# Attention's projections, output product and running sum computed from split operands; the scores stay unsplit products in 32-row groups

## The chip, the cores and the metric

One core of a Trainium2 chip runs the whole program. The metric is the device time of one execution in microseconds (us), median of the runs. The core has five engines with queues of their own: TensorE (PE in the rows, its weight loads PEld), VectorE (DVE), ScalarE (ACT), GpSimd (POOL) and SyncE (SP), which here only issues DMAs. An engine takes its instructions strictly in the order in which they were written, and waits on semaphores where another engine or a DMA has to be done first.

## What is computed

```python
x = x + 0.5 * ffn(layernorm(x))        # x: (8, 1024, 512), fp32
x = x + attn(layernorm(x))
x = x + 0.5 * ffn(layernorm(x))

def attn(x):                            # 16 heads of 32
    q = exp(split_heads(x @ Wq.T + bq)); k = exp(split_heads(x @ Wk.T + bk))
    v = split_heads(x @ Wv.T + bv)
    kv = cumsum(k[:, :, :, None] * v[:, :, None, :], axis=1)
    k1 = cumsum(k, axis=1)
    num = einsum('zsD,zsDd->zsd', q, kv)
    den = sum(q * k1, axis=-1, keepdims=True)
    return merge_heads(num / den) @ Wo.T + bo

def ffn(x):                             # 32 experts, each takes its 8 top tokens of a batch
    probs = softmax(x @ gate_w.T + gate_b, axis=tokens)
    vals, idx = top_k(probs, 8)         # per batch and expert
    merged = sum of the chosen tokens, weighted by vals
    h = gelu([merged, 1] @ w1[e]); o = [h, 1] @ w2[e]
    return scatter_add(o * vals at idx)
```

## The kernel before

The tokens are 64 tiles of 128 rows (`NT = 64`), eight tiles for each of the eight batches. The program has five stages: the gate of the first feed-forward part over all tiles, the 32 experts (`experts_*(…, 0)`), the attention stage, the 32 experts again (`experts_*(…, 1)`), and the final stage, which adds the experts' output and stores the result.

**Experts.** The weights, 2 MB for each quarter of an expert (a chunk, 128 chunks in a stage), are loaded by SyncE into a ring of SBUF slots of 4096 floats per partition (`load_chunk`, L498; `slot_of`, L190; `after_chunk`, L195). Slots 0 to 3 are the first 16,384 floats of SBUF. In the first expert stage `prepare_pe` and `prepare_act` (L609, L619) transpose the four attention weight matrices besides: ScalarE loads a matrix, TensorE transposes a quarter of it in each of 16 experts, and ScalarE copies the quarter into `WT`.

**Attention stage.** Every engine runs a loop over n (L684, L789, L850, L927), written as a software pipeline: the iteration n does the scores and the output of tile n, the projections of tile n + 1, the input normalisation of tile n + 2 and the second gate's logits of tile n - 1. c is n modulo 8, the tile's place in its batch. TensorE's order within an iteration is: AFTER product of tile n (skipped for c = 7; it completes the running sum of the keys in PSUM bank 2), transposes of K and Q, Q projection of n + 1, the 16 score products of tile n in 32-row groups, K projection, the residual product of n + 2, transposes of the tile for the second gate, V projection, the product with the running KV state (none for c = 0) and the 16 products scores times V, TRI product (running sum of the keys up to each row), KV outer product (none for c = 7), transposes of the normalised input of n + 2, output product with `WT[3]`, logits. A projection and the output product are four accumulated 128x128 by 128x512 fp32 products each (`project_pe`, L670; L771).

VectorE's order is (L850): bias to Q, normalise for the second gate, four score masks, bias to K, residual and statistics of n + 2, a step of the top-8 selection of the second gate (for n from 9 on, in four of eight iterations, `done` 0 to 3), normalise the input of n + 2 into `XN` (L895), then the denominator (multiply with bank 2, reduce, reciprocal, scale Q), KV mask, second residual `X2` and its statistics. ScalarE copies the transposes, exponentiates and copies V (L814), the attended tile `AT` (L820) and the transposed input `XT` (L824). GpSimd (L927): the power for the input normalisation, add `BO` to the residual (L935, which waits for `s_xn`, that is for L895), add up the KV state (L938), the power for the second normalisation. GpSimd's order is the order of these lines.

The V bias is not added to V; the product of bv with Wo is added to `BO` once at the start of the stage (L676 to L680, L838 to L840).

**Around the stage.** SyncE's `attention_sp` (L634) waits until the last chunk of the first expert stage is used (`s_used` 128), loads the tiles, and prefetches the chunks 128 and 129 at n = 1, chunk 130 at n = 62 and the biases and stored tiles at n = 63 and 64.

Of the kernel before, what the change touches and what calls it, by code (L numbers as in the profile page):

```python
# [20 lines left out]
def macaron_block(nc, x, Wq, bq, Wk, bk, Wv, bv, Wo, bo, gate_w, gate_b, w1, w2, out):  # L21
    F = mybir.dt.float32
    ALU = mybir.AluOpType
# [7 lines left out]

    x2d = nc.dram_tensor("x2_scratch", (B, S, D), F).ap()
# [5 lines left out]
    with ctx:  # L38
# [35 lines left out]
        BQ, BK, BO = (a.take(512) for _ in range(3))  # L74
        BVT = a.take(512)[:, 0:4]
# [16 lines left out]
        PR = TMP  # L92
        ath_at = a.at
        a.take(512)
# [8 lines left out]
        XT = [s.take(512).rearrange("p (k t) -> p k t", k=4) for _ in range(2)]  # L103
        Qs, Ks, Vs = ([s.take(512) for _ in range(2)] for _ in range(3))
        assert s.at <= 16384

        wt = Area(wth_at)
        WT = [wt.take(2048).rearrange("p (k n) -> p k n", k=4) for _ in range(4)]
        KT = B1
        AFTER = big[:, tri_at:tri_at + 128]  # L110
        AT = big2[:, ath_at - CUT:ath_at - CUT + 512]
# [4 lines left out]
        PT = [f.take(512) for _ in range(2)]  # L116
        wst = Area(qb_at)
# [40 lines left out]
        def sems(name, n):  # L158
            return [sem(f"{name}{i}") for i in range(n)]

        d_gw, d_gb, d_bias, d_b1, d_b2 = (sem(n) for n in ("d_gw", "d_gb", "d_bias", "d_b1", "d_b2"))
        d_xg, d_ring, d_wst = sems("d_xg", NX4), sems("d_ring", 8), sems("d_wst", 2)
# [3 lines left out]
        s_cst, s_tri, s_gwT, s_gt, s_obd0, s_bo, s_bo2 = (sem(n) for n in (  # L166
            "s_cst", "s_tri", "s_gwT", "s_gt", "s_obd0", "s_bo", "s_bo2"))
# [8 lines left out]
        s_used, s_hg, s_htT, s_ht, s_pt, s_sel, s_o, s_wT, s_wt_ = (sem(n) for n in (  # L176
            "s_used", "s_hg", "s_htT", "s_ht", "s_pt", "s_sel", "s_o", "s_wT", "s_wcopy"))

        s_resid, s_x1, s_x1st, s_x1ag, s_x1ve, s_x1rs, s_xn, s_x1b, s_xtT, s_xt = (sem(n) for n in (
            "s_resid", "s_x1", "s_x1st", "s_x1ag", "s_x1ve", "s_x1rs", "s_xn", "s_x1b", "s_xtT", "s_xt"))  # L180
        s_pq, s_pk, s_pv, s_qb, s_kb, s_v, s_qe, s_ke, s_ktT, s_kt, s_qtT, s_qt = (sem(n) for n in (
            "s_pq", "s_pk", "s_pv", "s_qb", "s_kb", "s_v", "s_qe", "s_ke", "s_ktT", "s_kt", "s_qtT", "s_qt"))
        s_S, s_st, s_av, s_at, s_upto, s_pr, s_red, s_rcp, s_qn, s_kv, s_kvm, s_kva = (sem(n) for n in (
            "s_S", "s_st", "s_av", "s_at", "s_upto", "s_pr", "s_red", "s_rcp", "s_qn", "s_kv", "s_kvm", "s_kva"))
# [5 lines left out]
        def slot_of(g):  # L190
            if g < 4 * E:
                return g if g < 7 else (g + 1) % 4
            return (0, 1, 7)[g - 4 * E] if g < 4 * E + 3 else (g - 1) % 4

        def after_chunk(g):  # L195
            if g < 4 * E:
                nxt = g + 7 if g < 4 else None if g < 7 else g + 4
            else:
                nxt = g + 5 if g < 4 * E + 2 else None if g == 4 * E + 2 else g + 4
            return nxt if nxt is not None and (nxt < 4 * E) == (g < 4 * E) and nxt < 8 * E else None  # L200
# [70 lines left out]
        def consts_act(act):  # L271
            act.wait_ge(s_cst, 16)
            nc.scalar.activation(AFTER, TRI, ACT.Identity, scale=-1.0, bias=1.0).then_inc(s_tri, 1)

# [315 lines left out]
        def experts_dve(dve, p):  # L590
            for e in range(E):
                x, i = E * p + e, e % 2
                dve.wait_ge(s_htT, x + 1)
                dve.wait_ge(s_used, 4 * x - 4)
                nc.vector.tensor_copy(HT[i], ps[:, 2 + i, :]).then_inc(s_ht, 1)  # L595
            dve.wait_ge(s_sel, E * p + E)
# [22 lines left out]
        def prepare_act(act, e):  # L619
# [5 lines left out]
            for m, kt, u in prepared(e):  # L625
                act.wait_ge(s_wT, u + 1)
                act.wait_ge(s_used, 7)
                nc.scalar.copy(WT[m][:, kt, :], ps[:, k, :]).then_inc(s_wt_, 1)
# [5 lines left out]
        def attention_sp(sp):  # L634
            def load_x1(n):
                sp.dma_start(X1[n % 4], xs[n]).then_inc(d_x1[n % 4], 16)

            sp.wait_ge(s_used, 4 * E)
            for n in range(4):
                load_x1(n)  # L640
            for n in range(-3, NT + 1):
# [28 lines left out]
        def project_pe(n, w, k):  # L670
            for j in range(4):
                t = mm(ps[:, k, :], XT[n % 2][:, j, :], WT[w][:, j, :], j == 0, j == 3)
            return t

        def attention_pe(pe):
            pe.wait_ge(s_wt_, 16)  # L676
            pe.wait_ge(d_bias, 16 * 7)
            for g in range(4):
                t = mm(ps[:, 1, :], BVT[:, g:g + 1].broadcast_to([128, 128]), WT[3][:, g, :], g == 0, g == 3)
            t.then_inc(s_bo, 1)  # L680
            pe.wait_ge(s_tri, 1)
            pe.wait_ge(s_o, 8)
            pe.wait_ge(s_bo2, 1)
            for n in range(-3, NT + 6):  # L684
# [4 lines left out]
                if live and c < 7:  # L689
                    pe.wait_ge(s_pr, n + 1)  # L690
                    mm(ps[:, 2, :], AFTER, Ks[i], False, False)
                if live:
# [4 lines left out]
                    pe.wait_ge(s_v, n + 1)  # L697
                    transpose4(5, Qs[i]).then_inc(s_qtT, 1)
                if nxt:
                    pe.wait_ge(s_xt, n + 2)  # L700
# [31 lines left out]
                if live:  # L732
                    pe.wait_ge(s_at, n)
# [26 lines left out]
                if 0 <= n + 2 < NT:  # L760
                    pe.wait_ge(s_xn, n + 3)
                    pe.wait_ge(s_xt, n + 2)
                    transpose4(7, XN).then_inc(s_xtT, 1)
                if n >= 9 and done == 3:
                    pe.wait_ge(s_at, min(n + 1, NT))
# [22 lines left out]
        def attention_act(act):  # L788
            for n in range(-3, NT + 6):  # L789
# [18 lines left out]
                if nxt:  # L808
                    act.wait_ge(s_kb, n + 2)
                    nc.scalar.activation(Ks[j], Ks[j], ACT.Exp).then_inc(s_ke, 1)  # L810
                    act.wait_ge(s_pv, n + 2)
                    act.wait_ge(s_av, n)
                    act.wait_ge(s_kv, kvs(n))
                    nc.scalar.copy(Vs[j], ps[:, 5, :]).then_inc(s_v, 1)  # L814
                if n >= 9 and done == 2:
                    topk_exp(act, 8 + gb)
                if live:
                    act.wait_ge(s_av, n + 1)
                    act.wait_ge(s_op, n)
                    nc.scalar.copy(AT, ps[:, 3, :]).then_inc(s_at, 1)  # L820
                if 0 <= n + 2 < NT:
                    act.wait_ge(s_xtT, n + 3)
                    act.wait_ge(s_pv, n + 1)
                    nc.scalar.copy(XT[n % 2], ps[:, 7, :].rearrange("p (k t) -> p k t", k=4)).then_inc(s_xt, 1)  # L824
# [12 lines left out]
        def attention_dve(dve):  # L837
            dve.wait_ge(d_bias, 16 * 7)  # L838
            dve.wait_ge(s_bo, 1)
            tt(BO, ps[:, 1, :], BO, ALU.add).then_inc(s_bo2, 1)  # L840
# [9 lines left out]
            for n in range(-3, NT + 6):  # L850
# [25 lines left out]
                if 0 <= n + 2 < NT:  # L876
# [5 lines left out]
                    stats(m % 2, X1[m % 4], s_x1, s_x1st, s_x1ag, s_x1ve, m)  # L882
                if n >= 9 and done == 0:
# [7 lines left out]
                if 0 <= n + 2 < NT:  # L891
# [4 lines left out]
                                            ALU.mult).then_inc(s_xn, 1)  # L896
                if nxt:
# [10 lines left out]
                       RDEN.unsqueeze(2).broadcast_to([128, 16, 32]), ALU.mult).then_inc(s_qn, 1)  # L908
                if live and c < 7:
# [15 lines left out]
        def attention_pool(pool):  # L925
            pool.wait_ge(s_bo2, 1)
            for n in range(-3, NT + 6):  # L927
                live = 0 <= n < NT
                c = n % 8
                if 0 <= n + 2 < NT:  # L930
# [4 lines left out]
                    nc.gpsimd.tensor_tensor(X1[m % 4], X1[m % 4], BO, ALU.add).then_inc(s_x1b, 1)  # L935
                if live and 0 < c < 7:
# [6 lines left out]
        def clear_pool(pool):  # L943
            pool.wait_ge(s_used, 4 * E + 3)
# [36 lines left out]
        def _(eng):  # L981
# [3 lines left out]
            for t_, s_ in ((BQ, bq), (BK, bk), (BO, bo)):  # L985
# [65 lines left out]
```

## Time and profile before

| | |
|---|---|
| median of 3 runs | 3023.77 us (3021.13 to 3023.98) |
| the profiled execution | 3021.42 us, its span 3019.3 us |
| mean granted TensorE clock | 0.949 of 2.4 GHz |
| busy over the span | TensorE 83%, VectorE 32%, ScalarE 17%, GpSimd 8% |
| chain that ended last | TensorE 62%, DMA 36% |
| stages (us from the start of the span) | gate 0 to 226, experts 226 to 772, attention 772 to 2305, experts 2305 to 2950, final 2950 to 3019 (roughly) |

In a row of a timeline the columns are: start, duration, engine, line, operation, output and input, count, and in brackets the idle time of the engine just before it and what ended it. A DVE or ACT start just behind a TensorE product shows when that product ended.

### The profile page before, as it was taken

How to read it: one execution, taken by the hardware profiler on the slowest of the kernel's cores; microseconds unless marked ns; L12 is line 12 of the kernel's file. 1: busy time of each engine (PE TensorE's matmuls, PEld its weight loads, DVE VectorE, ACT ScalarE, POOL GpSimd, SP SyncE). 2: the span in 40 equal slices, each digit the busy share in tenths (PEclk: the TensorE clock that was granted, in tenths of full speed). 3: DMA queues.
4: the chain of work that ended last, by engine and by line, in shares of the span. 5: the costliest groups of instructions: out<-in, count | busy, mean ns of one | idle time of the engine just before them, and what ended most of it. 6: DMA issues, size and time to landing. Idle time of an engine off the chain costs nothing.

```text
span 3019.3 us, 35156 instructions
## 1 busy us (share of the span) xinstructions
PE 2519.1 (83%) x15100; PEld 1157.3 (38%) x15100; DVE 968.5 (32%) x1793; ACT 518.8 (17%) x910; POOL 246.3 (8%) x278
## 2 busy tenths in 40 slices
PE   7866666666899999999999999999997666666668
PEld 4321121111355555555555555555553111111113
DVE  8600000000344554545545455454552000000006
ACT  7500000000122222222222222222221000000000
POOL 2100000000011111111111111111110000000000
PEclk9998888998999999999999999999998889988989
DMA  5699999999220000000000000000006999999999
GB/s 192 244 386 423 425 424 422 424 425 424 91 77 21 22 25 25 22 22 22 26 25 22 22 22 26 25 22 22 22 22 233 426 424 424 424 424 425 425 412 348
DMA packets 102841, 629.13 MB, mean 208 GB/s; under 512 B 9600, under 2 KB 9600, under 8 KB 53536
## 3 DMA queue, kind: packets, MB, share of 16 engines
q1 hardware_dynamic: 97696, 617.45, 50.2%
q10 hardware_dynamic: 4992, 9.44, 0.8%
q8 instruction: 120, 1.97, 0.3%
q14 instruction: 33, 0.27, 0.0%
HBM read 593.30 MB, written 33.55 MB: 208 GB/s over the span
## 4 chain that ended last, share of the span: by engine, by line
PE 62%; DMA 36%; DVE 1%; ACT 1%; issue 0%; SPq 0%; POOL 0%; DVEq 0%; ACTq 0%; POOLq 0%
PE ps L238 56%; DMA big<-in_L_ffn_w 35%; PE ps L242 5%; DMA big<-in_L_attn_Wq 1%; DVE big L246 1%; PE ps L342 0%; PE ps L316 0%; DMA big<-in_L_attn_x 0%; SPq L18 0%; DVE big L466 0%; ACT big L337 0%; ACT big L434 0%; DVE big L595 0%; POOL big L493 0%; PE ps L559 0%
## 5 line engine op out<-in xcount | busy, mean ns | idle before, releaser
L238 PE MATMUL ps<-big 128*32 128x512 f32 (+4 forms) x13304 | 2341.2, 500 | 444.1 <-DMA big<-in_L_ffn_w 377.4
L238 PEld LDWEIGHTS ps<-big 128*32 128x32 f32 (+2 forms) x13304 | 949.3, 148 | 1665.4 <-issue 1019.6
L246 DVE TENSOR_TENSOR big<-ps,big 128x512 f32<-128x512 f32 (+1 forms) x585 | 385.8, 687 | 721.8 <-PE ps L238 720.8
L595 DVE COPY big<-ps 128x512 f32<-128x512 f32 x64 | 44.2, 691 | 1201.8 <-PE ps L559 1201.8
L242 PE MATMUL ps<-big 128*128 128x128 f32 x1280 | 178.3, 277 | 19.3 <-ACT big L434 10.9
L242 PEld LDWEIGHTS ps<-big 128*128 128x128 f32 x1280 | 151.8, 142 | 92.6 <-issue 80.5
L933 POOL TENSOR_TENSOR big<-big 128x1 f32<-128x1 f32 x64 | 42.1, 657 | 1381.6 <-DVE big L848 1381.6
L583 ACT ACTIVATE big<-ps 128x512 f32<-128x512 f32 x64 | 38.2, 597 | 605.3 <-PE ps L238 605.3
L586 ACT COPY big<-ps 128x512 f32<-128x512 f32 x64 | 37.5, 585 | 557.6 <-PE ps L238 557.6
L844 DVE BATCH_NORM_STATS2 big<-big 128x6 f32<-128x512 f32 x128 | 88.9, 695 | 4.4
L807 ACT COPY big<-ps 128x512 f32<-128x512 f32 x64 | 37.5, 586 | 294.2 <-PE ps L242 294.2
L935 POOL TENSOR_TENSOR big<-big 128x512 f32<-128x512 f32 x64 | 81.1, 1268 | 56.5 <-DVE big L895 56.5
L938 POOL TENSOR_TENSOR big<-big 128x512 f32<-128x512 f32 x48 | 60.7, 1264 | 258.9 <-DVE big L246 258.9
L803 ACT ACTIVATE big<-big 128x512 f32<-128x512 f32 x64 | 40.4, 631 | 227.5 <-DVE big L246 227.5
L832 ACT ACTIVATE big<-ps,big 32x128 f32<-32x128 f32 x64 | 23.0, 359 | 249.0 <-PE ps L238 249.0
L246 DVE TENSOR_TENSOR big<-big 128x512 f32<-128x512 f32 (+1 forms) x80 | 63.7, 796 | 2.4
L814 ACT COPY big<-ps 128x512 f32<-128x512 f32 x64 | 37.5, 586 | 149.8 <-PE ps L238 149.8
L824 ACT COPY big<-ps 128x512 f32<-128x512 f32 x64 | 37.5, 586 | 118.4 <-PE ps L242 118.4
L941 POOL TENSOR_TENSOR big<-big 128x1 f32<-128x1 f32 x64 | 35.1, 549 | 252.8 <-DVE big L848 252.8
L559 PEld LDWEIGHTS ps<-big 128*128 128x128 f32 x256 | 40.5, 203 | 33.2 <-issue 30.0
L434 ACT ACTIVATE big<-big 128x512 f32<-128x512 f32 x64 | 49.3, 810 | 7.6 <-DVE big L459 7.4
L820 ACT COPY big<-ps 128x512 f32<-128x512 f32 x64 | 37.4, 585 | 73.4 <-PE ps L238 73.0
(54 smaller groups left out, 735.5 us busy)
## 6 DMA issues: line engine op xcount, KB each, us to landing
big<-in_L_ffn_w SPq DMA_DIRECT2D x256, 2048.0 KB, 17.6
big<-in_L_attn_x SPq DMA_DIRECT2D x16, 1024.0 KB, 8.8
big<-in_L_attn_x SPq DMA_DIRECT2D x64, 256.0 KB, 2.8
x_scratch<-big SPq DMA_DIRECT2D x64, 256.0 KB, 2.0
out_x<-big SPq DMA_DIRECT2D x64, 256.0 KB, 4.8
big<-x_scratch SPq DMA_DIRECT2D x44, 256.0 KB, 6.0
big<-x_scratch ACTq DMA_DIRECT2D x20, 256.0 KB, 6.6
big<-in_L_ffn_w SPq DMA_DIRECT2D x16, 64.0 KB, 4.9
```

The costliest lines, as they stand in the source:

```text
L238: return nc.tensor.matmul(o, l, r, start=start, stop=stop, skip_group_check=True)
L242: t = nc.tensor.transpose(ps[:, k, 128 * j:128 * j + 128], src[:, 128 * j:128 * j + 128], IDN[:, :])
L246: return nc.vector.tensor_tensor(o, p, q, op)
L434: nc.scalar.activation(XLA[h % NX4][:, j, :], XLA[h % NX4][:, j, :], ACT.Identity, bias=NMG[h % 2][:, j:j + 1], scale=RSG[h % 2][:, j:j + ...
L559: t = nc.tensor.transpose(ps[:, k, 128 * q:128 * q + 128], HG[i].rearrange("p (c t) -> p t c", t=4)[:, q, :], IDN[:, :])
L583: nc.scalar.activation(HG[i], ps[:, i, :], ACT.Gelu).then_inc(s_hg, 1)
L595: nc.vector.tensor_copy(HT[i], ps[:, 2 + i, :]).then_inc(s_ht, 1)
L803: nc.scalar.activation(Qs[j], Qs[j], ACT.Exp).then_inc(s_qe, 1)
L844: nc.vector.bn_stats(ST6[i], src).then_inc(s_st_, 1)
L933: nc.gpsimd.tensor_tensor(RS[m % 2], VE[m % 2], NHALF, ALU.pow).then_inc(s_x1rs, 1)
L935: nc.gpsimd.tensor_tensor(X1[m % 4], X1[m % 4], BO, ALU.add).then_inc(s_x1b, 1)
L938: nc.gpsimd.tensor_tensor(KV, KV, TMP, ALU.add).then_inc(s_kva, 1)
```

## The change

An operand of a product is held as two float32r parts: high part H = the value written as float32r, low part L = value - H, also written as float32r. A product A·B becomes three float32r products accumulated in PSUM: AH·BH + AH·BL + AL·BH. This is done for the three projections and the output product. The running sum (TRI, now `UPTO`, and `AFTER`) is a product with an exact 0/1 matrix and becomes two float32r products, with KH and KL. Score products, KV products, transposes, residual and logits stay fp32.

What comes with it:

- The weights' high parts stay in SBUF where `WT` was. Their low parts are computed by VectorE in the first expert stage (16 subtractions, `prepare_dve`), stored to DRAM by DMAs that ScalarE issues (16 of 256 KB), and loaded by SyncE at the start of the attention stage (4 MB) into ring slots 0 and 1. TensorE waits for them (`d_wl`) before its first product of the stage.
- Because slots 0 and 1 are taken, the chunks 128 and 129 are loaded at n = 62 and chunk 130 at n = 63.
- VectorE gains three 128x512 operations per tile: V plus its bias (in place of ScalarE's copy), the low part `ATL` of the attended tile, the low part `XTL` of the transposed input.
- ScalarE copies KH in place of V; GpSimd computes KL = K - KH.
- The start product of bv with Wo goes; bv is loaded by broadcast.

The diff, cut to its core:

```diff
         def attention_sp(sp):
+            sp.wait_ge(d_wls[0], 16 * 8)
+            sp.wait_ge(d_wls[1], 16 * 8)
+            sp.wait_ge(s_used, 4 * E)
+            for m in range(4):
+                sp.dma_start(WTL[m].bitcast(F), wl[m].rearrange("k p n -> p k n")).then_inc(d_wl, 16)
...
-                if n == 1:
+                if n == NT - 2:
+                    sp.wait_ge(s_pk, NT)
                     load_chunk(sp, 128)
+                    sp.wait_ge(s_resid, NT)
                     load_chunk(sp, 129)
-                if n == NT - 2:
-                    sp.wait_ge(s_resid, NT)
-                    load_chunk(sp, 130)
                     for m in range(16, 20):
                         load_f(sp, m)
                 if n == NT - 1:
                     sp.wait_ge(s_op, NT)
                     sp.wait_ge(s_kva, kvadds(NT))
+                    load_chunk(sp, 130)
                     load_biases(sp)
...
         def project_pe(n, w, k):
+            i = n % 2
             for j in range(4):
-                t = mm(ps[:, k, :], XT[n % 2][:, j, :], WT[w][:, j, :], j == 0, j == 3)
+                mm(ps[:, k, :], XTH[i][:, j, :], WTH[w][:, j, :], j == 0, False)
+                mm(ps[:, k, :], XTH[i][:, j, :], WTL[w][:, j, :], False, False)
+                t = mm(ps[:, k, :], XTL[i][:, j, :], WTH[w][:, j, :], False, j == 3)
             return t
...
                 if live and c < 7:
                     pe.wait_ge(s_pr, n + 1)
-                    mm(ps[:, 2, :], AFTER, Ks[i], False, False)
+                    mm(ps[:, 2, :], AFTER, KH, False, False)
+                    mm(ps[:, 2, :], AFTER, KL, False, False).then_inc(s_after, 1)
...
                 if nxt:
-                    pe.wait_ge(s_ke, n + 2)
                     pe.wait_ge(s_pr, n + 1)
-                    mm(ps[:, 2, :], TRI, Ks[(n + 1) % 2], (n + 1) % 8 == 0, False).then_inc(s_upto, 1)
+                    pe.wait_ge(s_kh, n + 2)
+                    mm(ps[:, 2, :], UPTO, KH, (n + 1) % 8 == 0, False)
+                    pe.wait_ge(s_kl, n + 2)
+                    mm(ps[:, 2, :], UPTO, KL, False, False).then_inc(s_upto, 1)
...
-                    pe.wait_ge(s_at, n + 1)
+                    pe.wait_ge(s_ath, n + 1)
                     for g in range(4):
-                        t = mm(ps[:, 1, :], h4(AT)[:, g, :], WT[3][:, g, :], g == 0, g == 3)
+                        mm(ps[:, 1, :], h4(ATH)[:, g, :], WTH[3][:, g, :], g == 0, False)
+                        mm(ps[:, 1, :], h4(ATH)[:, g, :], WTL[3][:, g, :], False, False)
+                    pe.wait_ge(s_atl, n + 1)
+                    for g in range(4):
+                        t = mm(ps[:, 1, :], h4(ATL)[:, g, :], WTH[3][:, g, :], False, g == 3)
                     t.then_inc(s_op, 1)
...
         attention_act
                     nc.scalar.activation(Ks[j], Ks[j], ACT.Exp).then_inc(s_ke, 1)
-                    act.wait_ge(s_pv, n + 2)
-                    nc.scalar.copy(Vs[j], ps[:, 5, :]).then_inc(s_v, 1)
+                    nc.scalar.copy(KH, Ks[j]).then_inc(s_kh, 1)
...
         attention_dve, behind the statistics of tile n + 2
+                if nxt:
+                    dve.wait_ge(s_pv, n + 2)
+                    tt(Vs[j], ps[:, 5, :], BV, ALU.add).then_inc(s_vb, 1)
         behind XN
+                if live:
+                    dve.wait_ge(s_ath, n + 1)
+                    dve.wait_ge(s_op, n)
+                    tt(ATL, ps[:, 3, :], ATH.bitcast(F), ALU.subtract).then_inc(s_atl, 1)
         behind the scaling of Q
+                if 0 <= n + 2 < NT:
+                    dve.wait_ge(s_xth, n + 3)
+                    dve.wait_ge(s_pv, n + 1)
+                    tt(XTL[n % 2], ps[:, 7, :]..., XTH[n % 2].bitcast(F), ALU.subtract).then_inc(s_xtl, 1)
...
         attention_pool, behind X1 + BO (L935)
+                if 0 <= n + 1 < NT:
+                    pool.wait_ge(s_kh, n + 2)
+                    pool.wait_ge(s_upto, n + 1)
+                    nc.gpsimd.tensor_tensor(KL, Ks[(n + 1) % 2], KH.bitcast(F), ALU.subtract).then_inc(s_kl, 1)
```

## Rows read from the trace of the kernel before

**Rows 1.** The page: busy time of TensorE and the granted clock in 40 slices.
```profile
PE 2519.1 (83%) x15100; PEld 1157.3 (38%) x15100; DVE 968.5 (32%) x1793; ACT 518.8 (17%) x910; POOL 246.3 (8%) x278
...
PEclk9998888998999999999999999999998889988989
```

**Rows 2.** Windows by stage: window, length, busy by engine, granted clock, DMA share, GB/s.
```profile
300.00:800.00 500.00, 328.97 (x1969) 96.74 (x1966) 27.95 (x43) 37.67 (x63) 1.81 (x2) 0.89 0.95 398
...
860.00:2240.00 1380.00, 1380.00 (x8382) 765.57 (x8381) 692.32 (x1280) 304.45 (x556) 203.34 (x222) 1.00 0.07 23
...
2300.00:2860.00 560.00, 355.96 (x2244) 100.89 (x2242) 26.22 (x40) 37.29 (x63) 4.06 (x2) 0.89 1.00 419
```

**Rows 3.** Line L797 by itself: ScalarE's first copy of each tile.
```profile
L797 ACT COPY big<-ps x64: 585/585/586, 805.0 to 2286.1; 128x512 f32<-128x512 f32 x64
```

**Rows 4.** Timeline of tile 18 (n = 18), from its K projection to its output product.
```profile
1229.70 0.19 PEld L238 LDWEIGHTS ps<-big 128*128 128x128 f32 x1 [0.24 <-issue]
...
1232.70 0.19 PEld L238 LDWEIGHTS ps<-big 128*128 128x128 f32 x1 [0.24 <-issue]
...
1237.01 0.55 DVE L895 TENSOR_SCALAR big<-big 128x512 f32<-128x512 f32 x1
...
1237.63 0.58 ACT L814 COPY big<-ps 128x512 f32<-128x512 f32 x1 [2.32 <-PE ps L238]
1237.63 1.27 POOL L935 TENSOR_TENSOR big<-big 128x512 f32<-128x512 f32 x1 [1.42 <-DVE big L895]
...
1239.56 0.58 ACT L820 COPY big<-ps 128x512 f32<-128x512 f32 x1 [1.35 <-PE ps L238]
...
1240.59 0.69 DVE L246 TENSOR_TENSOR big<-ps,big 128x512 f32<-128x512 f32 x1 [3.03 <-PE ps L238]
```

**Rows 5.** Groups by line and form: the selection's steps on VectorE, and GpSimd's add.
```profile
L308 DVE SCALAR_TENSOR_TENSOR big<-big 32x1024 f32<-32x1024 f32 x16 | 20.4, 1277 | 0.6
...
L282 DVE MAX8 big<-big 32x8 f32<-32x1024 f32 x16 | 19.5, 1216 | 4.9 <-ACT big L832 2.9 <-ACT big L444 1.7
L246 DVE TENSOR_TENSOR big<-big 32x1024 f32<-32x1024 f32 x16 | 19.4, 1215 | 0.2
L287 DVE MATCH_REPLACE8 big<-big 32x1024 f32<-32x1024 f32 x16 | 19.3, 1203 | 0.1
```

**Rows 6.** Timeline near the end of the attention stage, TensorE.
```profile
2289.35 0.63 PE L242 MATMUL ps<-big 128*128 128x128 f32 x4 [0.89 <-DVE big L246]
2291.14 3.73 PE L238 MATMUL ps<-big 128*128 128x128 f32 x40 [1.17 <-DVE big L246]
```

**Rows 7.** Windows around the same place.
```profile
2287.50:2291.10 3.60, 1.58 (x36) 1.18 (x32) 2.50 (x5) 0.58 (x1) 0.00 (x0) 1.00 0.98 380
2291.10:2294.60 3.50, 3.46 (x40) 3.13 (x40) 0.00 (x0) 0.00 (x0) 0.00 (x0) 0.51 1.00 400
```

**Rows 8.** Timeline in the first expert stage, TensorE, and the windows of that place.
```profile
651.10 2.78 PE L238 MATMUL ps<-big 128*32 128x512 f32 x24 [2.90 <-DMA big<-in_L_ffn_w]
655.99 3.49 PE L238 MATMUL ps<-big 128*32 128x512 f32 x16 [2.11 <-DMA big<-in_L_ffn_w]
...
651.00:655.00 4.00, 2.78 (x24) 0.68 (x24) 0.00 (x0) 0.59 (x1) 0.00 (x0) 1.00 1.02 434
655.00:658.50 3.50, 2.51 (x16) 0.59 (x16) 0.00 (x0) 0.00 (x0) 0.00 (x0) 0.67 0.95 405
```

**Rows 9.** DMA queue from 1000 to 2200 us: packets, MB, share of 16 engines.
```profile
q1 hardware_dynamic: 14688, 26.75, 6.9%
```

**Rows 10.** Timeline where the attention stage begins.
```profile
772.52 1.77 SPq L18 DMA_DIRECT2D big<-in_L_attn_x  x4
...
781.77 1.34 PE L238 MATMUL ps<-big 128*128 128x512 f32 x2 [3.19 <-DVE big L246]
```

**Rows 11.** SyncE's issues and DMA share where the attention stage ends.
```profile
2285.57 0.43 SPq L18 DMA_DIRECT2D big<-in_L_ffn_w  x1
...
2309.94 0.95 SPq L18 DMA_DIRECT2D big<-in_L_ffn_w  x2
...
2300.00:2310.00 10.00, 2.06 (x16) 1.28 (x13) 5.42 (x10) 2.11 (x4) 0.55 (x1) 0.91 0.65 194
2310.00:2330.00 20.00, 14.46 (x80) 4.96 (x84) 2.83 (x4) 3.26 (x6) 0.00 (x0) 0.62 1.02 404
```

More of the change, by code:

```diff
@@ L22, in macaron_block @@
     F = mybir.dt.float32
+    R = mybir.dt.float32r
     ALU = mybir.AluOpType
@@ L73, in macaron_block @@
         GT = a.take(128).rearrange("p (k e) -> p k e", k=4)
-        BQ, BK, BO = (a.take(512) for _ in range(3))
-        BVT = a.take(512)[:, 0:4]
+        BQ, BK, BV, BO = (a.take(512) for _ in range(4))
         SM = a.take(256)
@@ L92, in macaron_block @@
         PR = TMP
+        kh_at = a.at
+        a.take(1024)
         ath_at = a.at
-        a.take(512)
+        a.take(1024)
         assert a.at <= SIZE
@@ L102, in macaron_block, with halves @@
         X2, XN = s.take(512), s.take(512)
[L103 to L108, printed above, removed]
+        xt_at = s.at
+        s.take(2048)
+        Qs = [s.take(512) for _ in range(2)]
+        k_at = s.at
+        s.take(1024)
+        Vs = [s.take(512) for _ in range(2)]
+        assert s.at == 16384
+        def halves(name, at, n, dt=R):
+            return nc.alloc_sbuf_tensor_at(name, [128, n], dt, offset=base + 4 * at)
+        WTH = [halves(f"wth{m}", wth_at + 2048 * m, 2048)[:, :].rearrange("p (k n) -> p k n", k=4) for m in range(4)]
+        WTL = [halves(f"wtl{m}", 2048 * m, 2048)[:, :].rearrange("p (k n) -> p k n", k=4) for m in range(4)]
+        XTH = [halves(f"xth{i}", xt_at + 512 * i, 512)[:, :].rearrange("p (k t) -> p k t", k=4) for i in range(2)]
+        XTL = [halves(f"xtl{i}", xt_at + 1024 + 512 * i, 512)[:, :].rearrange("p (k t) -> p k t", k=4)
+               for i in range(2)]
         KT = B1
-        AFTER = big[:, tri_at:tri_at + 128]
-        AT = big2[:, ath_at - CUT:ath_at - CUT + 512]
+        ATH, ATL = (halves(f"at{i}", ath_at + 512 * i, 512)[:, :] for i in range(2))
+        Ks = [halves(f"keys{i}", k_at + 512 * i, 512, F)[:, :] for i in range(2)]
+        KH, KL = (halves(f"kh{i}", kh_at + 512 * i, 512)[:, :] for i in range(2))
+        UPTO, AFTER = (halves(f"tri{i}", tri_at + 128 * i, 128)[:, :] for i in range(2))
         f = Area(xn3_at)
@@ L116, in macaron_block @@
         PT = [f.take(512) for _ in range(2)]
+        WLS = [halves(f"wls{i}", f.at + 512 * i, 512)[:, :] for i in range(2)]
         wst = Area(qb_at)
@@ L272, in consts_act @@
             act.wait_ge(s_cst, 16)
+            nc.scalar.copy(UPTO, TRI).then_inc(s_tri, 1)
             nc.scalar.activation(AFTER, TRI, ACT.Identity, scale=-1.0, bias=1.0).then_inc(s_tri, 1)
@@ L627, in prepare_act, with prepare_dve @@
                 act.wait_ge(s_used, 7)
-                nc.scalar.copy(WT[m][:, kt, :], ps[:, k, :]).then_inc(s_wt_, 1)
+                nc.scalar.copy(WTH[m][:, kt, :], ps[:, k, :]).then_inc(s_wth, 1)
+                act.wait_ge(s_wls, u + 1)
+                act.dma_start(wl[m, kt], WLS[u % 2].bitcast(F)).then_inc(d_wls[u % 2], 16)
+        def prepare_dve(dve, e):
+            k = 2 + (e + 1) % 2
+            for m, kt, u in prepared(e):
+                dve.wait_ge(s_wth, u + 1)
+                dve.wait_ge(d_wls[u % 2], 16 * (u // 2))
+                tt(WLS[u % 2], ps[:, k, :], WTH[m][:, kt, :].bitcast(F), ALU.subtract).then_inc(s_wls, 1)
         def load_f(q, n):
@@ L984, in _ @@
             load_biases(sp)
-            for t_, s_ in ((BQ, bq), (BK, bk), (BO, bo)):
+            for t_, s_ in ((BQ, bq), (BK, bk), (BV, bv), (BO, bo)):
                 sp.dma_start(t_, s_.partition_broadcast(128)).then_inc(d_bias, 16)
-            for g in range(4):
-                sp.dma_start(BVT[:, g:g + 1], bv[128 * g:128 * g + 128].rearrange("(p a) -> p a", a=1)).then_inc(d_bias, 16)
             experts_sp(sp, 0)
```

71 lines of the change are left out of this document (35 added, 36 removed).

## The prediction

> **What bounds the kernel now.** I read the page first: TensorE is busy 83% of the span, no other engine a third of it, and the granted clock has dips at both ends and none in the middle [rows 1]. The windows by stage say why. In the two expert stages the DMA share is 0.95 to 1.00 at about 400 to 420 GB/s while TensorE is busy some 65%: the weights' transfer is the bound. In the attention stage from 860 to 2240 us TensorE is busy for 1380 of 1380 us at the full clock, 2.4 GHz, and the DMAs are idle 93% [rows 2]. So a product saved in the attention stage is a gain until something else makes TensorE wait, and a byte added in an expert stage is a loss. One tile costs (2286.1 - 805.0) / 63 = 23.51 us [rows 3].
>
> **Products.** An fp32 product of 512 columns leaves two records, each with its load. Eight loads of the K projection start in (1232.70 - 1229.70) / 7 = 0.429 us steps [rows 4], so a product takes 0.857 us. A record's 0.429 us is 1029 clocks at 2.4 GHz, two per column. No float32r product stands in the trace. Its bounds: above, the whole record, 0.429 us; below, 0.05 us, the mean of the 40 records of 128 columns that follow one another in 1.93 us (1239.56 - 1237.63 [rows 4]), which would need columns that cost nothing. I take one clock per column, half a record, 0.214 us: a part that is stored as a single value gives the array one pass over the columns, where the record of an fp32 product holds two. The load (0.19 us in a record [rows 4]) is then hidden by a hair instead of by half.
>
> "FP8 and Floating Point Precision" of the Trainium skill, section TensorE Precision Notes, states that true fp32 is four passes through the array and that reduced-precision fp32 reads four bytes and truncates them. By that page a float32r product is one of four passes, the 0.214 us again; no run here shows it.
>
> With it: projections and output product, 16 of 0.857 us become 48 of 0.214 us, 13.71 to 10.28 us per tile, 64 × 3.43 = 219.5 us. TRI, one product becomes two, 64 × 0.429 = 27.4 us. AFTER, 56 × 0.429 = 24.0 us. Together **-270.9 us** of TensorE work. The four products of bv with Wo at the start lay beside VectorE's sums: nothing.
>
> **Where TensorE waits next.** Of the added operations most have cover. VectorE gains 3 × 0.69 us, ScalarE none net, and each was idle over half the time in the attention stage (692 and 304 busy of 1380 us [rows 2]). The low part of the attended tile is needed only 8 products after its high part, 1.7 us later; the low part of the next input only after the output product. If that cover went, the price would be their 0.69 us per tile each.
>
> The low part of the keys has none. GpSimd does it behind X1 + BO, which waits for XN, and XN now stands on VectorE behind the new V bias, which waits for the V projection. Before, XN ran at 1237.01 us, ahead of the end of the V projection (ScalarE's copy at 1237.63 shows that end, 0.20 us earlier) [rows 4]. Counted from the end of the V projection:
> - 0.20 until VectorE starts, V bias 0.61 (0.69 less the overlap with the next), XN 0.55, 0.07, X1 + BO 1.27, KL 1.27 (the same shape as L935 [rows 4]), 0.13 to TensorE: 4.10 us.
> - TensorE's own work until it wants KL: state and V products 1.93 (1239.56 - 1237.63), then the first UPTO product. TRI with its change of shape took 1240.59 - 1239.56 = 1.03, that is 0.17 more than 0.857; so 0.17 + 0.21. Together 2.31 us.
>
> TensorE waits 1.8 us per tile, 63 × 1.8 = 113.4 us. Behind that wait are queued the KV outer product, the next input's transposes, the output product, and on VectorE the denominator; all of them move by the same time, none is added. In the first tile of a batch the state product (0.86 us) is absent and the wait that much longer: 7 × 0.86 = 6.0 us. And in four tiles of eight a step of the selection stands between V bias and XN: 1.22, 1.20 + 0.13 + 0.08, 1.22, or 1.28 + 0.15 less overlap, on average 1.3 us [rows 5], 28 tiles (n from 9 on): 36.4 us. Sum **+156 us**. Before, those steps ran while TensorE projected V.
>
> **The clock.** A wait of 3.1 us in the selection tiles and of 2.6 us in a batch's first tile also costs clock. Near the end of the stage TensorE idled 0.89 and 1.17 us around four transposes [rows 6]; the window before 2291.1 has TensorE 1.58 of 3.60 us busy at 1.00, the next 0.51, half rate, 1.2 GHz [rows 7]. The 40 products after it took 3.73 us; the same group takes 1.93 us in tile 18 [rows 6, 4]: one fall costs 1.8 us. In the expert stage 2.90 us idle were followed by four microseconds at 1.00, and 2.11 more by 0.67 [rows 8]: a wait of this length does it sometimes. I take one fall in each of the 28 selection tiles and in four of the seven first tiles, 32 × 1.8 = **+57.6 us**; none in the 1.8 us waits. Ends: 0 and one for each tile, 113.
>
> **The fixed costs.**
> - 16 stores of 256 KB, 4.19 MB, in the first expert stage, which the DMAs bound. In the middle of the run 26.75 MB took 6.9% of 1200 us × all 16 engines, so 323 GB/s at full share for this kind of packets [rows 9]: 13.0 us; at the stage's 424 GB/s 9.9 us. I take 12. The bias by broadcast adds 0.26 MB, 0.6 us. The subtractions and ScalarE's waits before its store lie in an expert's 20 us.
> - The load of the low parts: SyncE starts at 772.5 us, when it issued the tiles before; TensorE's first product came at 781.8 [rows 10]. 4 MB at the same rates end at 784 to 787 and the tiles queue behind them: 5.5 us (2 to 8).
> - At the end of the stage, chunks 128 and 129 now go at 2285.6, the place of 130, and 130 before the biases at 2300.5. DMAs are at 0.65 there and then saturated [rows 11]; what isn't moved before 2310 is moved at full price. One chunk of 2.10 MB, 4.9 us; both would be 9.8, none 0.
>
> Sum of the three 23.0 us.
>
> **The sum.** -270.9 + 156 + 57.6 + 23 = -34 us. The profiled execution is 3021.4 us (its span 3019.3), so 2987 us; the median of the runs lies 2.4 us above the profiled one: **2989 us**, faster by 1.1%. Over nine tenths of the product saving is given back. A measurement of this kernel tells differences over about 0.2% (6 us) from no change.
>
> **Rivals.**
> - *The clock holds through the waits.* For: 2.90 us idle left it at 1.00 [rows 8]. Then 57.6 us less: 2931 us. "TensorE: Matmul & The Clock Gate" of the Trainium skill, section "Why this matters for your kernels", has idle gaps between bursts throw the engine back to the lower clock. By that rule every top-k tile falls, which is my sum; the rows bear it out only in part.
> - *A float32r product costs more than a pass* (the other side). There are 48 × 64 + 2 × 64 + 2 × 56 = 3312 of them, so the decision falls at 0.214 + 34 / 3312 = 0.224 us, one hundredth more than I took. If a load of 0.19 us and its switch don't fit under the product, say 0.24 us, the result is near 3070; if two clocks per column are kept, 0.429 us, 3312 × 0.215 = 712 us more, near 3700. Against it: in those 40 records a load comes every 0.05 us on average, so loads as such keep up. That the split does nothing for the rate is this rival's upper end.
> - *The clock falls in every tile* (also slower): 63 falls instead of 32, 56 us more, 3045 us. Against: the fall at 2291 us came after 2.06 us idle with only four transposes between, and here 1.8 us lie between full work.
> - *KL isn't last*: if X1 + BO or XN got out before the V bias, the waits and falls go, 2776 us. The written order speaks against it.
>
> **Chances.** Forecast 0.57 (own range 2965 to 3015, of which a tenth within 0.2% of before); clock holds 0.19; product dearer 0.14; clock falls everywhere 0.07; no wait 0.03. Faster: 0.51 + 0.19 + 0.03 and a little from a product only slightly dearer, 0.74. Same 0.07, slower 0.19. The range runs from just under the holding clock, 2925, to the clock that falls everywhere, 3050; outside are the dear products and the case without a wait.
>
> **What would show it.** Float32r records in 0.21 us steps; GpSimd's KL ending 4 us behind the V projection; TensorE idle before L238 with GpSimd as releaser, about 1.8 us, 3 us where MAX8, MATCH_REPLACE8 or the mask precede XN; a granted clock in the attention stage of 0.9 to 1.0 where it was 1.00; a tile of about 21 to 24 us; the first expert stage longer by 10 to 13 us. Wrong: steps over 0.22 us, TensorE still without idle time, or waits released by VectorE.

## The result, and the profile after

The changed kernel takes 3044.38 us (median of 4 runs, 3043.04 to 3045.18), the kernel before 3022.68 us (4 runs). The ratio is 1.0072, interval [1.0054, 1.0089]: slower by 0.7%, where 1.1% faster was forecast. The time lies inside the stated range, on the other side of no change.

The page of the changed kernel, the lines that answer to [rows 1], and the chain by line:

```profile
PE 2386.7 (78%) x16116; PEld 1405.0 (46%) x16116; DVE 1104.7 (36%) x2000; ACT 523.1 (17%) x911; POOL 318.5 (10%) x342
...
PEclk9988899998799999999999999999988889889899
...
PE ps L257 40%; DMA big<-in_L_ffn_w 35%; PE ps L261 4%; POOL big L987 3%; POOL kh L991 3%; DVE big L884 1%; DVE big L920 1%; POOL big L985 1%; DMA big<-in_L_attn_Wq 1%; DVE big L886 0%; DMA wtl<-wl_scratch 0%; PE ps L336 0%; DVE big L888 0%; PE ps L362 0%; DVE big L265 0%
```

TensorE's busy time is 132 us less (2519.1 to 2386.7), and the program is longer. GpSimd, of which nothing stood in the chain worth a percent before, now has 6% of it, nearly all in two lines: L987 is the add of BO to the residual, L991 computes KL.

The windows, as in [rows 2] (window, length, busy by engine, granted clock, DMA share, GB/s), and the first copy of each tile, as in [rows 3]:

```profile
900.00:2200.00 1300.00, 1177.94 (x8743) 931.41 (x8742) 756.79 (x1365) 288.37 (x521) 250.35 (x262) 0.95 0.07 23
```
```profile
L839 ACT COPY big<-ps x64: 587/588/589, 823.9 to 2308.4; 128x512 f32<-128x512 f32 x64
```

In the attention stage TensorE is idle 9% of the time, where it was idle none, and the mean clock is 0.95, where it was 1.00. From tile to tile it is (2308.4 - 823.9) / 63 = 23.56 us, against 23.51 before: the product saving, forecast at 4.2 us a tile, has gone completely. The two traces split the 24.1 us between the spans at three marks. Up to SyncE's first issue for the attention stage: 772.5 before, 783.1 after, +10.6. From there to the first tile's copy: 32.5 and 40.8, +8.3. The 63 tiles: 1481.1 and 1484.5, +3.4. From the last tile's copy to the end: 733.2 and 735.0, +1.8.

A plain tile in the timeline of the changed kernel, what answers to [rows 4]:

```profile
1200.02 0.69 DVE L265 TENSOR_TENSOR big<-ps,big 128x512 f32<-128x512 f32 x1 [1.35 <-PE ps L257]
1200.63 0.54 DVE L938 TENSOR_SCALAR big<-big 128x512 f32<-128x512 f32 x1
1200.92 0.50 PE L257 MATMUL ps<-kh,tri 128*128 128x512 f32 x1
...
1201.25 1.27 POOL L987 TENSOR_TENSOR big<-big 128x512 f32<-128x512 f32 x1 [1.94 <-DVE big L938]
...
1202.47 1.26 POOL L991 TENSOR_TENSOR kh<-keys,kh 128x512 fp32r<-128x512 f32 x1
1203.79 0.50 PE L257 MATMUL ps<-kh,tri 128*128 128x512 f32 x1 [2.37 <-POOL kh L991]
```

One reads it downwards: V bias, XN, add, KL, then TensorE. The V projection ended 0.2 us before the first row, at 1199.8; KL is done at 1203.7, 3.9 us behind it. TensorE had put in its first UPTO product at 1200.92 and waited from there. This is the first tile of a batch (the state product is absent), so the wait is 2.37 us; in the tile before it is 1.49.

All waits of TensorE for KL, from the instructions that touch KH and KL:

```profile
L257 PE MATMUL ps<-kh,tri x240: 387/497/796, 816.2 to 2302.8; 128*128 128x512 f32 x120
its engine sat idle before it (us, times) until:
  POOL kh L991: 141.3, 63
```

And a selection tile, TensorE's timeline and the windows around it:

```profile
1223.59 0.50 PE L257 MATMUL ps<-kh,tri 128*128 128x512 f32 x1
1226.93 0.80 PE L257 MATMUL ps<-kh,tri 128*128 128x512 f32 x1 [2.85 <-POOL kh L991]
1227.53 1.91 PE L257 MATMUL ps<-big,keys 128*128 128x128 f32 x8
```
```profile
1221.00:1226.90 5.90, 3.09 (x45) 2.34 (x43) 3.15 (x4) 0.59 (x1) 2.56 (x3) 0.92 0.00 0
1226.90:1232.70 5.80, 5.76 (x20) 5.09 (x21) 3.62 (x6) 0.59 (x1) 0.38 (x1) 0.50 0.00 0
1232.70:1239.00 6.30, 6.30 (x36) 5.04 (x35) 1.72 (x4) 1.44 (x3) 1.45 (x2) 0.99 0.28 87
```

TensorE waits 2.85 us, and then works for 5.8 us at 0.50, half the clock: the eight KV records take 1.91 us where they take 1.05 at the full clock. That tile lasts 25.9 us.

The float32r products, by their loads in the K projection of the plain tile above:

```profile
1193.28 0.19 PEld L257 LDWEIGHTS ps<-wth,xtl 128*128 128x128 f32 x1
1193.51 0.19 PEld L257 LDWEIGHTS ps<-wth,xth 128*128 128x128 f32 x1
...
1195.34 0.19 PEld L257 LDWEIGHTS ps<-wth,xtl 128*128 128x128 f32 x1
```

Nine steps from 1193.28 to 1195.34 are 0.229 us each, not 0.214.

### The profile page after: what moved, and what is told of

It reads as the page before. It is cut to its first block, busy times and chain, and to the rows that moved or that the text cites. A ratio compares the mean times of both kernels' runs of the same rounds, so it can differ in the third digit from the quotient of the medians.

```text
span 3043.4 us, 37630 instructions
## 1 busy us (share of the span) xinstructions
PE 2386.7 (78%) x16116; PEld 1405.0 (46%) x16116; DVE 1104.7 (36%) x2000; ACT 523.1 (17%) x911; POOL 318.5 (10%) x342
## 4 chain that ended last, share of the span: by engine, by line
PE 45%; DMA 37%; POOL 6%; issue 6%; DVE 5%; ACT 0%; SPq 0%; POOLq 0%; DVEq 0%; ACTq 0%
PE ps L257 40%; DMA big<-in_L_ffn_w 35%; PE ps L261 4%; POOL big L987 3%; POOL kh L991 3%; DVE big L884 1%; DVE big L920 1%; POOL big L985 1%; DMA big<-in_L_attn_Wq 1%; DVE big L886 0%; DMA wtl<-wl_scratch 0%; PE ps L336 0%; DVE big L888 0%; PE ps L362 0%; DVE big L265 0%
## 5 line engine op out<-in xcount | busy, mean ns | idle before, releaser
L257 PE MATMUL ps<-big 128*32 128x512 f32 (+3 forms) x10560 | 1271.1, 491 | 456.7 <-DMA big<-in_L_ffn_w 385.3
L257 PEld LDWEIGHTS ps<-big 128*32 128x32 f32 (+2 forms) x10560 | 482.6, 137 | 1149.2 <-DMA big<-in_L_ffn_w 556.3
L257 PE MATMUL ps<-wth,xth 128*128 128x512 f32 x768 | 320.1, 417 | 1.4 <-DVE xtl L265 1.4
L257 PE MATMUL ps<-wtl,xth 128*128 128x512 f32 x768 | 301.6, 393 | 0.0
L257 PE MATMUL ps<-wth,xtl 128*128 128x512 f32 x768 | 300.6, 391 | 0.0
L257 PE MATMUL ps<-wth,at 128*128 128x512 f32 x512 | 193.2, 439 | 0.8 <-ACT at L862 0.8
L257 PEld LDWEIGHTS ps<-wth,xth 128*128 128x128 f32 x768 | 145.2, 189 | 34.3 <-DVE xtl L265 1.8
L257 PEld LDWEIGHTS ps<-wth,xtl 128*128 128x128 f32 x768 | 145.1, 189 | 32.1
L257 PEld LDWEIGHTS ps<-wtl,xth 128*128 128x128 f32 x768 | 145.7, 190 | 24.3 <-issue 0.5
L606 ACT COPY big<-ps 128x512 f32<-128x512 f32 x64 | 37.6, 587 | 553.1 <-PE ps L257 553.1
L987 POOL TENSOR_TENSOR big<-big 128x512 f32<-128x512 f32 x64 | 81.1, 1267 | 161.5 <-DVE big L938 161.5
```

The source lines that it names most:

```text
L257: return nc.tensor.matmul(o, l, r, start=start, stop=stop, skip_group_check=True)
L606: nc.scalar.copy(PT[i], ps[:, 4 + i, :]).then_inc(s_pt, 1)
```

## The experiments

The theory (A) after this reading: three things eat the saving, the wait for KL (141 us), the falls of the clock in it, and a float32r product that costs 0.015 us more than a pass over its columns (3312 × 0.015 = 50 us). The rivals (B) differ by experiment. Each run is compared with the kernel before on the same chip, whose median was 3022.8 us beside e1 to e4 and 3023.2 us beside e5 to e8.

**e1: KL ahead of the add.** In GpSimd's loop:

```diff
                     nc.gpsimd.tensor_tensor(RS[m % 2], VE[m % 2], NHALF, ALU.pow).then_inc(s_x1rs, 1)
-                    pool.wait_ge(s_xn, m + 1)
-                    nc.gpsimd.tensor_tensor(X1[m % 4], X1[m % 4], BO, ALU.add).then_inc(s_x1b, 1)
                 if 0 <= n + 1 < NT:
                     pool.wait_ge(s_kh, n + 2)
                     pool.wait_ge(s_upto, n + 1)
                     nc.gpsimd.tensor_tensor(KL, Ks[(n + 1) % 2], KH.bitcast(F), ALU.subtract).then_inc(s_kl, 1)
+                if 0 <= n + 2 < NT:
+                    pool.wait_ge(s_xn, m + 1)
+                    nc.gpsimd.tensor_tensor(X1[m % 4], X1[m % 4], BO, ALU.add).then_inc(s_x1b, 1)
```

> The changed kernel with one order changed: GpSimd computes the keys' low part KL ahead of the residual's add of BO, not behind it. Theory A (TensorE waits in every tile for KL, which stands behind V bias, XN and the add, 141 us in all, and its clock falls in the long waits, some 160 us at half rate): both go, the 63 tiles take about 1265 instead of 1484.5 us, the total is 2810 to 2850, the granted clock in the attention stage is 1.00. Rival B (another wait stands right behind it: VectorE's low parts, or the longer float32r products alone make up the loss): 2960 or more, TensorE idle by VectorE or ScalarE.

Measured: 2820.15 us, ratio 0.9327 [0.9311, 0.9342]. The stage's window and the same tile reading:

```profile
900.00:2050.00 1150.00, 1149.10 (x9099) 915.00 (x9094) 777.32 (x1421) 299.52 (x542) 261.63 (x271) 1.00 0.08 27
```
```profile
L257 PE MATMUL ps<-kh,tri x240: 387/402/505, 813.9 to 2076.0; 128*128 128x512 f32 x120
its engine sat idle before it (us, times) until:
  POOL kh L989: 0.8, 1
  DVE big L265: 0.3, 1
```
```profile
L839 ACT COPY big<-ps x64: 586/587/588, 817.6 to 2081.6; 128x512 f32<-128x512 f32 x64
```

TensorE is busy 1149.1 of 1150 us at the full clock, and no other wait takes the place of this one. 63 tiles take 1264.0 us, 20.06 each. So the place of one GpSimd instruction is worth 224 us of the total, and the change as a whole is 7% faster than before when it stands elsewhere.

**e2: work in the wait.** TensorE gets seven products of no use between the two UPTO products:

```diff
                     mm(ps[:, 2, :], UPTO, KH, (n + 1) % 8 == 0, False)
+                    if n >= 1:
+                        pe.wait_ge(s_xt3, n)
+                    for _ in range(7):
+                        mm(ps[:, 4, :], UPTO, WTH[0][:, 0, :], True, True)
                     pe.wait_ge(s_kl, n + 2)
```

> The changed kernel with seven float32r products of no use (512 columns, to bank 4, 7 x 0.23 = 1.6 us) between the two UPTO products of each tile, in the time in which TensorE waits for KL. Theory A (part of the loss is the clock that falls in the wait): nothing on the path gets longer, since the wait is 1.5 us or more, and the falls go or get few; 45 to 75 us faster than the changed kernel, 2970 to 3000, attention clock above 0.98. Rival B (the falls cost nothing, as TensorE waits anyway): 3040 to 3060, with the clock up or not.

Measured: 2979.51 us, ratio 0.9856 [0.9841, 0.9871], 65 us less than the changed kernel.

```profile
L843 ACT COPY big<-ps x64: 586/587/588, 819.9 to 2240.0; 128x512 f32<-128x512 f32 x64
```
```profile
900.00:2200.00 1300.00, 1259.13 (x9523) 989.98 (x9522) 789.70 (x1426) 300.97 (x545) 262.68 (x273) 1.00 0.08 24
```

More work on the bounding engine, and the program is faster. KL comes as late as before; what goes is the half clock (1.00 instead of 0.95). TensorE still idles 43.6 us before the second product, in 37 tiles, 1.9 us ahead of the first tile's copy and pieces of up to 1.5 us behind it, and these cost no clock. Plain tiles last 21.8 us in both, so the added products cost nothing there. The three traces then price the tiles: 1484.5 us with wait and falls, 1420.1 with the wait alone, 1264.0 without. The falls cost 64.4 us, the wait 156.1. The idle row shows less, as it counts the product before the wait as busy for 0.50 us, where the next one starts 0.34 us behind it when nothing is waited for (e1); and the product behind the wait takes 0.34 us to its successor instead of 0.23.

**e3: the running sum undone** (TRI and AFTER as fp32 products of the whole keys; KH, KL and their instructions gone):

```diff
-                    pe.wait_ge(s_kh, n + 2)
-                    mm(ps[:, 2, :], UPTO, KH, (n + 1) % 8 == 0, False)
-                    pe.wait_ge(s_kl, n + 2)
-                    mm(ps[:, 2, :], UPTO, KL, False, False).then_inc(s_upto, 1)
+                    pe.wait_ge(s_ke, n + 2)
+                    mm(ps[:, 2, :], TRI, Ks[(n + 1) % 2], (n + 1) % 8 == 0, False).then_inc(s_upto, 1)
```

> The changed kernel with the running sum of the keys undone: TRI and AFTER are fp32 products of the whole keys again, no KH and KL. Projections and output product stay split. Theory A: TensorE's work grows by 0.40 us for each of 64 TRI and 56 AFTER products, 48 us, and the wait (141 us) and the falls of the clock (about 65 us) go: 2860 to 2900. Rival B (the low parts that VectorE makes, or the float32r products themselves, hold the stage up): 3040 to 3100.

Measured: 2868.48 us, ratio 0.9486 [0.9472, 0.95]. Against e1 it is 48.3 us more, the 48 us of the fp32 products. Splitting the sum costs the changed kernel 176 us as it stands, and gains 48 us with KL in its right place.

**e4: the products' step by themselves** (before the attention stage, all of no use):

```diff
+            for _ in range(40):
+                mm(ps[:, 7, :], WTH[0][:, 0, 0:128], WTH[1][:, 0, :], True, True)
+            for _ in range(24):
+                mm(ps[:, 7, 0:256], WTH[0][:, 1, 0:128], WTH[1][:, 0, 0:256], True, True)
...
+            for _ in range(24):
+                mm(ps[0:64, 7, :], WTH[0][:, 2, 0:64], WTH[1][:, 0, :], True, True)
...
```

> The changed kernel with a series of products of no use before the attention stage, all into bank 7, for their step alone: float32r of 512 columns (40), 256 (24), 512 with the low parts (24), 512 with 64 columns of weights (24), 384 (24), fp32 of 512 (12). The time grows by some 40 us. Theory A (a fixed cost per float32r product at full clock, of the change of weights): steps of 0.229, 0.122, 0.229, 0.229 or less with the narrow weights, 0.175 us; narrow weights at 0.214 would say that the load is what shows. Rival B (a lower rate per column, 0.448 ns instead of 0.417): 0.229, 0.115, 0.229, 0.229, 0.172. fp32: 0.429 per record.

```profile
795.19 14.68 PE L257 MATMUL ps<-wth,wth 128*128 128x512 f32 x64 [11.51 <-DMA wtl<-wl_scratch]
809.71 5.63 PE L257 MATMUL ps<-wtl,wtl 128*128 128x512 f32 x24
815.17 9.87 PE L257 MATMUL ps<-wth,wth 128*64 128x512 f32 x48
824.88 11.32 PE L257 MATMUL ps<-big 128*128 128x512 f32 x26
```

From 809.71 to 815.17 are 24 products of 512 columns, 0.2275 us each, with the low parts as operands. The groups before and behind hold two forms each; by the starts of the single records in the trace the steps are 0.120 us for 256 columns, 0.173 for 384, 0.227 for 512, 0.229 for 512 with 64 columns of weights, and 0.429 for each fp32 record. From 256 to 512 columns a column costs 0.107 / 256 = 0.418 ns, one clock of 2.4 GHz, and 0.013 us are left over whatever the width. So it is a fixed cost per product, as A had it, and not B's lower rate, which would make 0.115 us of 256 columns. Half the columns of weights shorten the load's record from 0.19 to 0.13 us and don't lower the step, so it isn't the length of the load. Each of these products has a load of its own, so whether the cost comes with the change of weights, as A said, or with the product isn't shown: what it is stays open. (One run, 3084.07 us, 40 us over the changed kernel, as the series is long.)

**e5: no low parts through DRAM** (on top of e1; the products that take a weight's low part take its high part, in the projections and the output product, so the low part's contribution is left out and that of the high part is added twice: the number of products is the same, the values are not):

```diff
-            for m in range(4):
-                sp.dma_start(WTL[m].bitcast(F), wl[m].rearrange("k p n -> p k n")).then_inc(d_wl, 16)
...
-                act.dma_start(wl[m, kt], WLS[u % 2].bitcast(F)).then_inc(d_wls[u % 2], 16)
...
-                mm(ps[:, k, :], XTH[i][:, j, :], WTL[w][:, j, :], False, False)
+                mm(ps[:, k, :], XTH[i][:, j, :], WTH[w][:, j, :], False, False)
```

> e1_kl_first without the weights' low parts going through DRAM: no stores in the first expert stage, no load at the start of the attention stage, and the products that take a weight's low part take its high part instead (so the low parts' contribution is left out). The same number of products. Theory A (the fixed costs are real: the first expert stage is bound by its DMAs, and TensorE waits for the low parts at the start; the two traces show 10.6 and 8.3 us): 17 to 21 us faster than e1_kl_first, 2799 to 2803 beside its 2820. Rival B (they were in the shade of other waits): within 5 us of e1_kl_first.

Measured: 2808.49 us, 11.7 us less than e1: between the theories, and nearer to A. SyncE's first issue for the attention stage comes at 775.8 instead of e1's 781.7, 5.9 us; from there to the first tile's copy it is 30.9 us instead of 36.0, 5.1. The load of the low parts at the start thus costs 5.1 us. The stores cost some 6 us, not the 10.6 by which the traces before and after differ there: the kernel is the same up to this issue in all the traces with the stores, and it stands anywhere from 779.8 (e7) to 783.5 us (e6) in them, 781.8 in the mean of eight. The 3.3 us between 772.5 before and 775.8 here are less than this scatter.

**e6: V bias behind XN** (GpSimd's order as in the change):

```diff
-                if nxt:
-                    dve.wait_ge(s_pv, n + 2)
-                    tt(Vs[j], ps[:, 5, :], BV, ALU.add).then_inc(s_vb, 1)
...
                     nc.vector.tensor_scalar(XN, X1[m % 4], MV[m % 2][:, 0:1], RS[m % 2], ALU.subtract,
                                             ALU.mult).then_inc(s_xn, 1)
+                if nxt:
+                    dve.wait_ge(s_pv, n + 2)
+                    tt(Vs[j], ps[:, 5, :], BV, ALU.add).then_inc(s_vb, 1)
```

> The changed kernel with VectorE's V bias moved behind XN, the other link of the chain; GpSimd's order as in the change. Theory A (KL is late because XN stands behind the V bias): XN starts with the statistics, 0.6 us before the V projection ends, KL is done some 2.7 us behind that end instead of 4.1, TensorE wants it at 2.3: a wait of 0.4 us in a plain tile, 1.2 in a selection tile, some 60 us in place of 141, hardly a fall of the clock: 2870 to 2910. Rival B (only GpSimd's order counts, XN was not late): 3030 or more.

Measured: 2879.14 us, ratio 0.9522 [0.9506, 0.9537].

```profile
L257 PE MATMUL ps<-kh,tri x240: 387/497/796, 815.9 to 2137.6; 128*128 128x512 f32 x120
its engine sat idle before it (us, times) until:
  POOL kh L991: 44.2, 63
```
```profile
900.00:2050.00 1150.00, 1114.10 (x8704) 876.67 (x8706) 752.71 (x1363) 286.26 (x518) 254.15 (x260) 1.00 0.08 26
```

The chain has two ends from which it can be shortened. From this one it takes away 97 us of the idle time and the falls, and leaves a wait of 0.7 us a tile in the mean: 0.2 in a plain tile, 0.6 to 1.2 in one with selection, 1.1 in the first of a batch.

**e7: fp32 products in the changed kernel** (each group of three as one product of the high parts, in the output product too, which then waits for ATL as a whole; the low parts are left out of the value):

```diff
-                mm(ps[:, k, :], XTH[i][:, j, :], WTH[w][:, j, :], j == 0, False)
-                mm(ps[:, k, :], XTH[i][:, j, :], WTL[w][:, j, :], False, False)
-                t = mm(ps[:, k, :], XTL[i][:, j, :], WTH[w][:, j, :], False, j == 3)
+                t = mm(ps[:, k, :], XTH[i][:, j, :].bitcast(F), WTH[w][:, j, :].bitcast(F), j == 0, j == 3)
...
```

> The changed kernel with each group of three float32r products in projections and output product made one fp32 product of the high parts (the low parts are left out of the value); all copies, low parts, waits and DMAs stay. Theory A (a float32r product costs 0.229 us, so a split product saves 0.857 - 0.687 = 0.170 us, and the wait for KL is counted from the V projection's end whatever it is made of): 1024 x 0.170 = 174 us slower than the changed kernel, 3200 to 3230. Rival B (longer products would take up the wait for KL): 3100 or less.

Measured: 3214.0 us, ratio 1.0629 [1.0613, 1.0644], 169.6 us more than the changed kernel. (The falls cost less here, with a mean granted clock of 0.96 from the first to the last tile against 0.95, so this isn't the price of the products alone.) The wait is the same to the tenth:

```profile
L257 PE MATMUL ps<-kh,tri x240: 389/497/798, 813.9 to 2463.5; 128*128 128x512 f32 x120
its engine sat idle before it (us, times) until:
  POOL kh L986: 141.3, 63
```

A wait that is counted from the end of a TensorE group doesn't shrink when that engine has more to do before it.

**e8: the start of the stage** (on top of e1):

```diff
...
+            for n in range(4):
+                load_x1(n)
             for m in range(4):
                 sp.dma_start(WTL[m].bitcast(F), wl[m].rearrange("k p n -> p k n")).then_inc(d_wl, 16)
-            for n in range(4):
-                load_x1(n)
...
             pe.wait_ge(s_tri, 2)
-            pe.wait_ge(d_wl, 64)
             pe.wait_ge(s_o, 8)
...
                     pe.wait_ge(s_L3, n - 1)
+                    pe.wait_ge(d_wl, 64)
                     project_pe(n + 1, 0, 0).then_inc(s_pq, 1)
```

> e1_kl_first, and at the start of the attention stage SyncE loads the first tiles ahead of the weights' low parts, and TensorE waits for the low parts only before the first projection, not before the residual products. Theory A (of the start's 8.3 us most is a wait that the first tile's residual, normalisation and transposes, 7.8 us in the trace, can lie beside): 5 to 8 us faster than e1_kl_first, 2812 to 2815. Rival B (the load of the low parts ends later as the tiles go first, and the start is bound by it as before): within 2 us of e1_kl_first.

Measured: 2816.9 us, ratio 0.9316 [0.9302, 0.933], 3.3 us less than e1 and the fastest of the runs that compute all three parts of each product: less than the 5 to 8 us of A, more than B's 2.

```profile
791.21 2.05 PE L257 MATMUL ps<-big 128*128 128x512 f32 x2 [5.90 <-DVE big L265]
...
799.88 0.77 PE L257 MATMUL ps<-wth,xth 128*128 128x512 f32 x1 [2.25 <-DMA wtl<-wl_scratch]
```

The residual product comes 8.5 us behind SyncE's first issue (782.76 to 791.21), in e1 13.8 us (781.66 to 795.42), but the first projection still waits 2.25 us for the low parts: the load is longer than what was put beside it. Of the 5.3 us 4.0 are left at the first tile's copy (32.0 us behind the first issue, 36.0 in e1) and 3.3 in the total.

## Why the prediction was wrong

**What bounds the kernel, and the wait: right.** The wait for KL was found at its place with its chain (V bias, XN, add, KL), and its size, 156 us, is what e1 and e2 give, 156.1. It isn't a lucky sum either. By the first copies of the tiles the wait lengthens a plain tile by 1.78 us (19.99 in e1, 21.77 in the changed kernel; 1.8 forecast) and the first of a batch by 2.66 (19.10 and 21.76; 1.8 + 0.86 forecast), and a selection tile by 2.7 to 3.4 (e1 and e2; 3.1 forecast). That it moves with the V projection's end and not with TensorE's work is e7.

**The clock: right in kind, a little small.** 57.6 us forecast, 64.4 measured (e2). The rival in which the clock holds is refuted, and so is the one in which it falls in every tile: plain tiles with 1.5 us of idle time stayed at the full clock. Of the 64 tiles it falls in all 28 with selection (n % 8 from 1 to 4, n of 9 and more), where TensorE has one wait like the 2.85 us above, and in two first tiles of a batch; I had counted 28 and 4, at 1.8 us each, and 64.4 us for 30 falls are 2.1 each. The selection tiles' waits are 2.6 to 3.1 us. A first tile's is 2.4, and there the clock fell in two of eight, but in e7 in all eight behind a wait just as long, so that count was a guess. In the tiles of e1, e2 and e6 there is no fall.

**The price of a float32r product: the step that failed.** I took 0.214 us; it is 0.229. The prediction had named the point from which this decides, 0.224, had steps over 0.22 us as a sign of being wrong, and put 0.14 on the rival "costs more than a pass"; it decided. 3312 × 0.015 = 50 us of product saving weren't there: 220 in place of 271. As a check, e1's 63 tiles save 1481.1 - 1264.0 = 217 us of work. With fp32 in place of the three parts (e7) the program is 169.6 us longer, where 0.857 - 3 × 0.229 = 0.170 us in each of 1024 products makes 174. By e4 it is a fixed cost per product on top of one clock per column. The one pass was right, then; that rate times columns was all of the price was assumed, and the change makes three products out of one, so that a fixed cost comes 3312 times.

The page "FP8 and Floating Point Precision" of the Trainium skill (TensorE Precision Notes) has four passes for true fp32. The trace agrees, if a float32r product is one of them: a quarter of 0.857 us is 0.418 ns for each of 512 columns. The page says nothing of the fixed part.

**The fixed costs: the sum came near by luck.** 23.0 forecast, 10.6 + 8.3 + 1.8 = 20.7 between the traces. The stores alone are nearer 6 us (e5) than 12, so that term was twice too large. The load of the low parts is right, 5.1 (e5) for 5.5. The 8.3 us of the start hold something else besides, which the forecast didn't have: with KL in its right place (e1) the start takes 36.0 us instead of 40.8, so 4.8 us of it are the wait for KL and a fall of the clock ahead of the first tile's copy. The end can't tell 1.8 from 4.9: from the last tile's copy on, the nine traces with the change take 735.0 to 739.1 us, against 733.2 before.

The terms put right give the result: 2989 + 50 + 7 - 2 = 3044 us, and 3044.4 was measured. (The 7 and the 2 are differences of the same traces; the 50 is worked out from the step alone, so it is the term that this sum tests.) The sum was a difference of 271 and 237 us. Errors that are small in each term, 15 ns in a product, are as large as such a difference; the sign deserved less confidence than 0.74.

## What to carry to other kernels

When an operation on an engine with little to do is added to a chain on the bounding engine, its place in that engine's order is part of its price: behind an instruction that waits for something late, the idle engine stops the busy one (here 224 us for one instruction of 1.26 us). Write down for each new operand what it stands behind, not only what it needs. And where a change multiplies the number of instructions, measure the step of one before counting on the rate: per-instruction costs that don't show in the old form show three times over in the new one.

## What the runs showed of the hardware

A float32r product of 512 columns takes 0.227 to 0.229 us at the full clock, 0.013 to 0.016 more than its columns; an fp32 record of the same width, which takes two clocks for each column, 0.429, only 0.002 more than its 1024 clocks. At half the clock the excess is gone: in the changed kernel's first projection nine products start from 805.43 to 808.85 us in eight steps of 0.427 us, which is 512 clocks of 1.2 GHz.

```profile
805.43 0.63 PE L257 MATMUL ps<-wtl,xth 128*128 128x512 f32 x1
...
808.85 0.63 PE L257 MATMUL ps<-wth,xth 128*128 128x512 f32 x1
```

"TensorE: Matmul & The Clock Gate" of the Trainium skill, section "Back-to-back issue gap", gives columns divided by 2.4 GHz plus 2.5 ns when warm, and columns divided by 1.2 GHz when not. The fp32 records, taken as two passes, and the half-clock steps agree; the float32r products at the full clock are 13 to 16 ns from their columns, five to six times what it says.

And idle time isn't free on an engine whose clock follows its work: filling 1.6 us of each wait with products of no use made the kernel 65 us faster (e2).
